# Cross-attention: other key tiles for the value jobs, and one later step of the next mask

## The chip, the cores and the metric

The kernel runs on one core of a Trainium2 chip. The metric is the time of one execution in microseconds (us), measured on the device; of the kernel before there are three such runs. "Layer 0" and "layer 1" are the two decoder layers.

## The reference, cut to what matters

The program is a two-layer pre-norm decoder on x of 4 x 512 x 256 in float32. In each layer come self-attention, cross-attention over a context of 4 x 1601 x 192, and a mixture of experts. Only the two cross-attentions are touched. In layer 0 (8 heads of 64) it is, for each batch element,

```
q = (x @ W_q).reshape(b, n, 8, 64); k, v = (context @ W_k), (context @ W_v)
sim  = einsum('bihd,bjhd->bhij', q, k) / 8
sim  = where(mask[:, None, None, :], sim, -max)
attn = softmax(sim); out = einsum('bhij,bjhd->bihd', attn, v)
return out @ W_o + b_o
```

with n = 512 queries, j = 1601 keys, and x = x + this of layernorm(x). Layer 1 is the same with 16 heads and no mask.

## The kernel before, in words

`cross(layer)` works in groups: one group is two heads of one batch element. Layer 0 has 16 groups (4 for each batch element), layer 1 has 32 (8 for each). A group runs over 13 key tiles of 128 keys (the last has 65), numbered t = 0 to 12, and a closing step t = 13. All five engines walk the same static list of groups and tiles, each in its own queue and in program order, and meet only at semaphores. There is no planner: what is done when is given by the function `at(g, t)`, which names the jobs that follow the scores of tile t in group g, and by `maxima_at`, which places the maxima.

Main work of a tile t of group g:

- TensorE makes the scores of the two heads (L1122 and L1123, two matmuls each), ScalarE takes their exponential into a ring PR (L1234), and GpSimd adds the exponentials up over the tiles into ACC (L1009), for the softmax's denominator.
- After every second tile, at even t, TensorE multiplies the exponentials of two tiles with the values V (L1139, eight matmuls at t = 2, 4, ..., 12, four at t = 13). So an even tile holds much more TensorE work than an odd one.
- In tiles 1 to 11 TensorE also makes plain scores for group g + 1 (L1075), of which VectorE takes the row maxima (L1292 in layer 0, L1295 in layer 1). The banks that hold them are few: TensorE may write the next only when VectorE has reduced an earlier one. In layer 1 an odd tile has two such pairs (one between the two heads' scores, one after the jobs), an even tile has one (after the jobs). In layer 0 every tile has three single ones (tile 4 has four).

Jobs, which share two banks in turn:

- `k` (t = 0 to 3) and `q` (t = 0) project keys and queries of group g + 1. ScalarE copies the rounded part, VectorE subtracts it (L1263, L1268, L1270), and DMAs place the parts.
- `sum` (t = 2) adds ACC over the partitions (L1047). It waits until the second last job's bank is free, which is a `k` job whose bank VectorE frees at L1263.
- `v` projects the values of four heads, two key tiles to a job: ten matmuls of 256 columns (L1039), then one copy on ScalarE (L1182). The seventh job has one key tile, five matmuls; it is called the short job below. Seven jobs serve two groups. `values_at(g)` says which a group has: four and then three in the next group, or, where a new batch element begins, none and then all seven. The last groups have none.
- `out` (t = 10, 11) projects the output of group g - 1; `row` (t = 12) turns the maxima of g + 1 into a row.
- VectorE inverts the denominators of group g - 1 (L1302, tiles 4 to 7 in layer 0, two each at tiles 5 and 7 in layer 1) and normalises at tiles 8 and 9 (L1309).

In layer 0 VectorE prepares the next batch element's mask in the second of its four groups, in four steps, `mask_step(b, c)`. Step 0 casts the columns of the mask (L1326) and then its rows, 128 x 1601 bytes to bfloat16 (L1327), and releases the DMA that loads the next rows. Step 1 reduces (L1330) and scales (L1331), step 2 makes the per-key bias and the scale of the queries (L1333, L1334), step 3 makes what is added ahead of the maxima (L1336). They are used two groups later at the earliest. Before the change step 0 stands at t = 0, and steps 1, 2, 3 at t = 11, 12, 13. That happens in groups 1, 5 and 9 of layer 0, counted from 0.

The value jobs stand at t = 4 and on, one to a tile, without a gap: three jobs at 4, 5, 6; four at 4 to 7; seven at 4 to 10.

Of the kernel before, what the change touches and what calls it, by code (L numbers as in the profile page):

```python
# [14 lines left out]
B, S, C = 4, 512, 256  # L15
# [41 lines left out]
class Core:  # L57
# [716 lines left out]
    def cross(self, layer):  # L774
# [6 lines left out]
        heads, masked = HEADS[layer], layer == 0  # L781
        pairs = heads // 2
# [14 lines left out]
        def values_at(g):  # L797

            n = g // 2 + 1  # L800
            if n >= G // 2:
                return []
            jobs = [("v", n, c) for c in range(len(VJ))]
            if 2 * n % pairs == 0:
                return jobs if g % 2 == 1 else []
            return jobs[0:4] if g % 2 == 0 else jobs[4:]

        def at(g, t):

            jobs = []  # L810
            if g + 1 < G:
                jobs += {0: [("k", g + 1, 0), ("q", g + 1, 0)], 1: [("k", g + 1, 1)], 2: [("k", g + 1, 2)],
                         3: [("k", g + 1, 3)]}.get(t, [])
            if g >= 1 and t == 2:
                jobs.append(("sum", g - 1, 0))
            if t >= 4:
                jobs += values_at(g)[t - 4:t - 3]
            if g >= 1 and t in (10, 11):
                jobs.append(("out", g - 1, t - 10))
            if g + 1 < G and t == 12:  # L820
                jobs.append(("row", g + 1, 0))
            return jobs

        after = [("sum", G - 1, 0), ("out", G - 1, 0), ("out", G - 1, 1)]
        order = before() + [("row", 0, 0)] + [x for g in range(G) for t in range(KT + 1) for x in at(g, t)] + after
        place = {x: i for i, x in enumerate(order)}

# [8 lines left out]
        def maxima_at(g, t, *at):  # L836

            return [(g + 1, *x) for w, b in zip(where, blocks) for x in b if w[0] == t and w[1] in at] if g + 1 < G else []
# [6 lines left out]
        with self.room() as sb:  # L845
# [50 lines left out]
            with self.stage() as (sem, ctx):  # L896
# [348 lines left out]
                def _(dve):  # L1245
                    steps = [0]

                    def link(ins):

                        steps[0] += 1  # L1250
                        ins.then_inc(o_step, 1)
                        dve.wait_ge(o_step, steps[0])

                    def job(x):
                        kind, g, c = x
                        i, par = place[x], g % 2
                        J = JB[i % 2]
                        if kind == "k":
                            o, w = CHUNKS[c]
                            dve.wait_ge(k_high, NC * g + c + 1)  # L1260
                            for h in range(2):
                                hd = slice(h * DH, (h + 1) * DH)
                                last = dve.tensor_tensor(KB[0:DH, par, h, o:o + w], J[hd, 0:w], KH[hd, o:o + w], ALU.subtract)  # L1263
                            last.then_inc(job_done[i % 2], 1)
                        elif kind == "q":
                            sc = qscale[:, g // pairs:g // pairs + 1]
                            dve.wait_ge(q_high, g + 1)
                            dve.scalar_tensor_tensor(QA[DH:P, par, 0, :], J[0:DH, :], sc[0:DH], QZ[0:DH, 0, :],  # L1268
                                                     ALU.mult, ALU.subtract)
                            dve.scalar_tensor_tensor(QA[0:DH, par, 1, :], J[DH:P, :], sc[DH:P], QZ[DH:P, 1, :],  # L1270
                                                     ALU.mult, ALU.subtract).then_inc(job_done[i % 2], 1)
                        elif kind == "out":
                            dve.wait_ge(job_ready[i % 2], i // 2 + 1)
                            dve.wait_ge(x_based, B * NT)
                            t = g // pairs * NT + 2 * c
                            x2 = X[:, t:t + 2, :]
                            dve.tensor_tensor(x2, J[:, :].rearrange("p (t n) -> p t n", t=2), x2, ALU.add)\
                               .then_inc(job_done[i % 2], 1)

                    def maximum(g, i, h):  # L1280

                        t, c = i % NT, i // NT
                        o, w = CHUNKS[c]
                        w = min(w, S2 - o)
                        if not masked and h == 0:
                            return
                        out = mx[:, h, t, c:c + 1]
                        dve.wait_ge(mx_ready, 2 * (NT * NC * g + i) + h + 1)
                        m = 2 * i + h
                        if masked:  # L1290
                            b = MX[(m if g == 0 else h) % 4][:, 0:w]
                            dve.tensor_tensor_reduce(b, b, maskadd[:, g // pairs % 2, o:o + w], 1.0, -BIG,  # L1292
                                                     ALU.add, ALU.max, out).then_inc(mx_done, 1)
                        else:
                            dve.tensor_reduce(mx[:, :, t, c], couples[i % 2 if g == 0 else 0][:, :, 0:w], AX.X, ALU.max).then_inc(mx_done, 1)  # L1295

                    def invert(g, i):

                        if i == 0:
                            wait_job(dve, ("sum", g, 0))  # L1300
                        part = RD[:, i * P:(i + 1) * P]
                        dve.reciprocal(part, part).then_inc(inverted, 1)  # L1302
# [8 lines left out]
                    def maxima_end(g):  # L1311
                        dve.wait_ge(mx_done, (2 if masked else 1) * NT * NC * (g + 1))
                        if g >= 1:
                            wait_ready(dve, ("row", g - 1, 0))
                        dve.tensor_reduce(MT[:, 0:8], mx[:, :, :, :].rearrange("p h t c -> p (h t) c"), AX.X, ALU.max).then_inc(m_ready, 1)

                    def mask_step(b, c):

                        if not masked:
                            if b == 0 and c == 0:  # L1320
                                dve.memset(qscale[:, :], DH ** -0.5).then_inc(prep, 1)
                            return
                        seen, scale, add = allowed[:, 0, b:b + 1], allowed[:, 1, b:b + 1], maskadd[:, b % 2, 0:S2]
                        if c == 0:
                            dve.wait_ge(self.cross_in, 32 + 16 * b)
                            link(dve.tensor_copy(keybias[:, b, :], mask_cols[:, b, :]))  # L1326
                            dve.tensor_copy(add, mask_rows[:, :]).then_inc(rows_read, 1)  # L1327
                            dve.wait_ge(rows_read, b + 1)
                        elif c == 1:
                            link(dve.tensor_reduce(seen, add, AX.X, ALU.max))  # L1330
                            link(dve.tensor_scalar(scale, seen, BIG, None, ALU.mult))  # L1331
                        elif c == 2:
                            link(dve.tensor_scalar(keybias[:, b, :], keybias[:, b, :], -1.0, scale, ALU.add, ALU.mult))  # L1333
                            dve.tensor_scalar(qscale[:, b:b + 1], seen, DH ** -0.5, None, ALU.mult).then_inc(prep, 1)  # L1334
                        else:
                            link(dve.tensor_scalar(add, add, -1.0, scale, ALU.add, ALU.mult))  # L1336
# [29 lines left out]
                    for g in range(G):  # L1366
                        for t in range(KT + 1):
                            for x in maxima_at(g, t, 0, 1, 2, 3):
                                maximum(*x)
                            if t == max(where)[0] and g + 1 < G:  # L1370
                                maxima_end(g + 1)
                            for x in at(g, t):
                                job(x)
                            if g >= 1:
                                for i in parts_at.get(t, ()):
                                    invert(g - 1, i)
                                if t in (8, 9):
                                    normalise(g - 1, t - 8)
                            if masked and g % pairs == 1 and g // pairs + 1 < B and t in (0, 11, 12, 13):
                                mask_step(g // pairs + 1, (0, 11, 12, 13).index(t))  # L1380
                    for i in range(NT):
                        invert(G - 1, i)
                        if i % 2 == 1:
# [501 lines left out]
```

## Time and profile before

| | us |
|---|---|
| median of 3 runs | 3261.02 |
| lowest, highest | 3252.44, 3264.88 |
| the profiled execution | 3253.24 |
| its span | 3251.5 |

The page of the profile gives each engine's busy time. Its view of stretches gives, for each stretch of the span that is named by its start and end, the stretch's length, and then for PE (TensorE's matmuls), PEld (its weight loads), DVE (VectorE), ACT (ScalarE) and POOL (GpSimd) the busy time in it with the number of instructions, then the mean granted clock of TensorE (1.00 is 2.4 GHz, 0.50 is 1.2 GHz), the busy share of the DMA engines and the rate. The stretches below are tiles or runs of tiles: each begins with the first score matmul (L1122) of its first tile and ends where that of the next begins, so the length of a stretch is what TensorE's queue needed for it. A timeline row gives the start, the duration, engine, line, operation and tiles, and in brackets the idle time before it and what ended that.

### The profile page before, as it was taken

How to read it: one execution, taken by the hardware profiler on the slowest of the kernel's cores; microseconds unless marked ns; L12 is line 12 of the kernel's file. 1: busy time of each engine (PE TensorE's matmuls, PEld its weight loads, DVE VectorE, ACT ScalarE, POOL GpSimd, SP SyncE). 2: the span in 40 equal slices, each digit the busy share in tenths (PEclk: the TensorE clock that was granted, in tenths of full speed). 3: DMA queues.
4: the chain of work that ended last, by engine and by line, in shares of the span. 5: the costliest groups of instructions: out<-in, count | busy, mean ns of one | idle time of the engine just before them, and what ended most of it. 6: DMA issues, size and time to landing. Idle time of an engine off the chain costs nothing. (4 is left out here: it accounts for less than half of the span.)

```text
span 3251.5 us, 38293 instructions
## 1 busy us (share of the span) xinstructions
PE 2838.1 (87%) x12634; PEld 1750.4 (54%) x12634; DVE 1856.3 (57%) x3758; ACT 1303.4 (40%) x2329; POOL 1660.1 (51%) x1408
## 2 busy tenths in 40 slices
PE   5578886999899999685799999999999999999979
PEld 5323334556565565443555656555565556556557
DVE  2456674666766665435556555555655565565546
ACT  1135554445454454120344444444444444444410
POOL 0344302666666667501366666666666666666710
PEclk8779998999999999795799999999999999999979
DMA  8666603232332321000322322322332232222110
GB/s 281 145 163 153 143 1 95 64 100 53 97 71 52 91 69 31 33 0 0 99 63 65 71 81 67 72 56 60 95 73 49 67 102 59 60 62 69 31 52 27
DMA packets 113533, 245.81 MB, mean 76 GB/s; under 512 B 15366, under 2 KB 61703, under 8 KB 112184
## 3 DMA queue, kind: packets, MB, share of 16 engines
q1 hardware_dynamic: 107128, 219.82, 27.0%
q0 software_dynamic: 5696, 23.42, 2.6%
q8 instruction: 102, 1.67, 0.2%
q14 instruction: 95, 0.78, 0.1%
q10 hardware_dynamic: 512, 0.13, 0.0%
HBM read 107.31 MB, written 31.76 MB: 43 GB/s over the span
## 5 line engine op out<-in xcount | busy, mean ns | idle before, releaser
L1009 POOL TENSOR_TENSOR ACC<-ACC,PR 128x512 f32<-128x512 f32 (+1 forms) x1056 | 1331.0, 1283 | 486.3 <-ACT PR L1234 477.3
L1234 ACT ACTIVATE PR<-banks 128x512 f32<-128x512 f32 (+1 forms) x832 | 468.8, 597 | 682.7 <-PE banks L1123 681.6
L1295 DVE TENSOR_REDUCE mx<-banks 128x2 f32<-128x800 f32 (+1 forms) x512 | 504.2, 986 | 406.5 <-PE banks L1075 405.3
L1139 PE MATMUL banks<-PR,V 128*64 128x512 f32 (+1 forms) x2496 | 602.9, 607 | 0.0
L1122 PE MATMUL banks<-QA,KA 128*128 128x512 f32 (+1 forms) x1248 | 535.5, 429 | 8.5 <-DMA QB<-ROW 7.3
L1075 PE MATMUL banks<-KH,QZ 128*128 128x400 f32 (+1 forms) x1536 | 482.9, 372 | 58.0 <-DVE mx L1295 37.8
L1123 PE MATMUL banks<-QB,KB 65*128 65x512 f32 (+1 forms) x1248 | 494.9, 397 | 0.0
L1075 PEld LDWEIGHTS banks<-KH,QZ 128*128 128x128 f32 x1536 | 268.5, 189 | 246.5 <-issue 113.9
L1234 ACT ACTIVATE PR<-banks,small 128x512 f32<-128x512 f32 (+1 forms) x416 | 269.4, 687 | 306.9 <-PE banks L1123 299.2
L1292 DVE CUSTOM_DVE_ANT_0 banks<-banks,maskadd 128x400 f32<-128x400 f32 (+1 forms) x512 | 289.8, 587 | 158.9 <-PE banks L1075 153.4
L1263 DVE TENSOR_TENSOR KB<-banks,KH 64x400 fp32r<-64x400 f32 (+1 forms) x384 | 219.4, 571 | 260.7 <-ACT KH L1167 255.2
L1122 PEld LDWEIGHTS banks<-QA,KA 128*128 128x128 f32 (+1 forms) x1248 | 231.0, 185 | 220.3 <-issue 188.9
L1139 PEld LDWEIGHTS banks<-PR,V 128*64 128x64 f32 (+1 forms) x2496 | 154.6, 137 | 262.6 <-issue 243.3
L1009 POOL TENSOR_TENSOR ACC<-PR 128x512 f32<-128x512 f32 x96 | 121.1, 1280 | 340.8 <-ACT PR L1234 340.8
L1123 PEld LDWEIGHTS banks<-QB,KB 65*128 65x128 f32 (+1 forms) x1248 | 231.5, 185 | 32.2 <-issue 11.0
L1027 PE MATMUL banks<-CX,WK 128*128 128x400 f32 (+1 forms) x960 | 220.6, 361 | 14.2 <-DVE KB L1263 6.3
L1039 PE MATMUL banks<-WV,CX 128*128 128x256 f32 (+1 forms) x1560 | 210.8, 280 | 0.0
L1039 PEld LDWEIGHTS banks<-WV,CX 128*128 128x128 f32 (+1 forms) x1560 | 204.5, 184 | 11.6
L676 ACT ACTIVATE PR<-banks 128x512 f32<-128x512 f32 x256 | 144.5, 600 | 154.9 <-DVE banks L746 127.9
L1027 PEld LDWEIGHTS banks<-CX,WK 128*128 128x128 f32 x960 | 178.5, 194 | 47.2 <-DVE QA L1270 17.7
L1302 DVE RECIPROCAL RD<-RD 128x128 f32<-128x128 f32 x192 | 172.5, 928 | 36.4 <-ACT RD L1159 35.4
L717 DVE CUSTOM_DVE_ANT_0 banks<-banks,strip 128x512 f32<-128x512 f32 x176 | 119.3, 706 | 30.5 <-PE banks L587 29.0
(241 smaller groups left out, 2975.8 us busy)
## 6 DMA issues: line engine op xcount, KB each, us to landing
KA<-KH SPq DMA_DIRECT2D x192, 400.5 KB, 6.7
CX<-ctx_split SPq DMA_DIRECT2D x8, 2403.0 KB, 10.7
WK<-wk_split SPq DMA_DIRECT2D x48, 256.0 KB, 5.7
WV<-wv_split SPq DMA_DIRECT2D x24, 512.0 KB, 3.7
QA<-QZ SPq DMA_DIRECT2D x96, 128.0 KB, 2.3
QB<-QZ SPq DMA_DIRECT2D x96, 128.0 KB, 2.3
first<-in_w_in SPq DMA_DIRECT2D x8, 1024.0 KB, 6.1
second<-in_w_out1T SPq DMA_DIRECT2D x8, 1024.0 KB, 8.8
```

Of the source, the lines that this page charges most:

```text
L1009: pool.tensor_tensor(acc, other, PR[0:r, n % RING, :], ALU.add).then_inc(summed, 1)
L1027: last = pe.matmul(J[:, 0:w], W[:, u, :], CX[:, v, o:o + w], start=(n == 0), stop=(n == 4))
L1039: last = pe.matmul(J[0:r, o:o + 2 * P], CX[:, v, t * P:t * P + r], WV[:, u, :], start=(n == 0), stop=(n == 4))
L1075: pe.matmul(bank_at[:, 0:w], QZ[:, h, t * P:(t + 1) * P], KH[:, o:o + w], start=True, stop=True).then_inc(mx_ready, 1)
L1122: pe.matmul(SB[n % 3][0:r, :], KA[:, par, h, t * P:t * P + r], QA[:, par, h, :], start=True, stop=False)
L1123: pe.matmul(SB[n % 3][0:r, :], KB[:, par, h, t * P:t * P + r], QB[:, par, h, :], start=False, stop=True).then_inc(sc_ready, 1)
L1139: last = pe.matmul(OB[h * DH:(h + 1) * DH, :], V[0:r, g % 4, s, h * DH:(h + 1) * DH], PR[0:r, (n + h) % RING, :], start=(s == 0), stop=(s ...
L1234: act.activation(PR[0:r, n % RING, :], SB[n % 3][0:r, :], ACT.Exp, bias=keybias[0:r, g // pairs, t:t + 1] if masked else 0.0).then_inc(pro ...
L1263: last = dve.tensor_tensor(KB[0:DH, par, h, o:o + w], J[hd, 0:w], KH[hd, o:o + w], ALU.subtract)
L1292: dve.tensor_tensor_reduce(b, b, maskadd[:, g // pairs % 2, o:o + w], 1.0, -BIG, ALU.add, ALU.max, out).then_inc(mx_done, 1)
L1295: dve.tensor_reduce(mx[:, :, t, c], couples[i % 2 if g == 0 else 0][:, :, 0:w], AX.X, ALU.max).then_inc(mx_done, 1)
L1302: dve.reciprocal(part, part).then_inc(inverted, 1)
```

## The change: what it does

```diff
@@ at(g, t), the jobs of a tile
-            if t >= 4:
-                jobs += values_at(g)[t - 4:t - 3]
+            todo = values_at(g)
+            for x, tile in zip(todo, {0: (), 3: (5, 7, 9), 4: (4, 5, 7, 9), 7: range(4, 11)}[len(todo)]):
+                if tile == t:
+                    jobs.append(x)
@@ VectorE's queue, at the end of a tile
-                            if masked and g % pairs == 1 and g // pairs + 1 < B and t in (0, 11, 12, 13):
-                                mask_step(g // pairs + 1, (0, 11, 12, 13).index(t))
+                            if masked and g % pairs == 1 and g // pairs + 1 < B:
+                                for c in {11: (0,), 12: (1, 2), 13: (3,)}.get(t, ()):
+                                    mask_step(g // pairs + 1, c)
```

A group with three value jobs has them at tiles 5, 7 and 9, one with four at 4, 5, 7 and 9, one with seven where they were. Mask step 0 moves from tile 0 to the end of tile 11, step 2 from tile 12 stays there behind step 1, which moves from 11 to 12, and step 3 stays at 13. The order of the jobs among themselves, and so the bank of each, stays the same.

## Rows read from the trace of the kernel before

**Rows 1.** The page: busy time of the engines, and the largest group.

```profile
PE 2838.1 (87%) x12634; PEld 1750.4 (54%) x12634; DVE 1856.3 (57%) x3758; ACT 1303.4 (40%) x2329; POOL 1660.1 (51%) x1408
...
L1009 POOL TENSOR_TENSOR ACC<-ACC,PR 128x512 f32<-128x512 f32 (+1 forms) x1056 | 1331.0, 1283 | 486.3 <-ACT PR L1234 477.3
```

**Rows 2.** Stretches, layer 1, tiles 4 to 9: group without value jobs, with three, four.

```profile
1906.36:1925.47 19.11, 16.61 (x67) 8.60 (x67) 13.74 (x16) 7.18 (x13) 15.11 (x13) 1.00 0.82 235
2048.91:2069.20 20.29, 18.81 (x93) 11.75 (x92) 13.71 (x16) 8.67 (x16) 15.14 (x13) 1.00 0.44 100
2001.26:2022.43 21.17, 20.29 (x108) 13.63 (x107) 13.72 (x16) 9.57 (x17) 15.19 (x13) 1.00 0.43 97
```

**Rows 3.** Stretches, layer 1: tile 4, 5, 9, each without and with a job.

```profile
1906.36:1910.10 3.74, 3.50 (x15) 1.36 (x15) 3.14 (x4) 1.43 (x3) 3.70 (x4) 1.00 0.66 134
2001.26:2005.70 4.44, 4.44 (x26) 2.62 (x25) 3.14 (x4) 2.02 (x4) 3.91 (x4) 1.00 0.68 139
1910.10:1912.76 2.66, 2.04 (x11) 1.51 (x9) 0.99 (x1) 1.19 (x2) 1.32 (x2) 1.00 0.97 219
2005.70:2008.65 2.95, 2.95 (x20) 2.77 (x19) 0.99 (x1) 1.36 (x3) 1.42 (x2) 1.00 1.02 232
1922.75:1925.47 2.72, 2.01 (x10) 1.51 (x9) 1.54 (x3) 1.19 (x2) 1.46 (x2) 1.00 0.40 170
1971.22:1974.17 2.95, 2.95 (x21) 2.77 (x19) 0.99 (x1) 1.37 (x3) 1.42 (x2) 1.00 0.00 0
```

**Rows 4.** Timeline, layer 1, tiles 6 and 7 without jobs: maxima after the scores.

```profile
1914.01 0.63 PE L1075 MATMUL banks<-KH,QZ 128*128 128x400 f32 x2 [0.15 <-DVE mx L1295]
...
1918.61 0.63 PE L1075 MATMUL banks<-KH,QZ 128*128 128x400 f32 x2 [0.62 <-DVE mx L1295]
```

**Rows 5.** Stretches, layer 0, tiles 4 to 9: group without value jobs, with three, four.

```profile
871.32:890.59 19.27, 16.34 (x69) 9.04 (x68) 15.31 (x44) 8.31 (x13) 13.95 (x12) 1.00 0.80 235
824.85:844.84 19.99, 18.96 (x93) 12.16 (x93) 15.32 (x44) 9.78 (x16) 13.97 (x12) 1.00 0.45 103
772.35:793.06 20.71, 20.45 (x108) 14.07 (x108) 15.42 (x44) 10.70 (x17) 14.04 (x12) 1.00 0.44 99
```

**Rows 6.** Stretches, layer 0: tile 4, 5, 9, each without and with a job.

```profile
871.32:876.44 5.12, 4.01 (x17) 1.91 (x17) 3.46 (x10) 1.85 (x3) 3.42 (x3) 1.00 0.69 140
772.35:777.48 5.13, 5.13 (x28) 3.21 (x28) 3.45 (x10) 2.45 (x4) 3.44 (x3) 1.00 0.69 140
876.44:878.97 2.53, 1.75 (x9) 1.23 (x9) 2.33 (x6) 1.34 (x2) 1.02 (x1) 1.00 1.01 235
777.48:780.13 2.65, 2.65 (x18) 2.47 (x18) 2.46 (x7) 1.34 (x2) 1.15 (x1) 1.00 0.99 232
888.58:890.59 2.01, 1.75 (x9) 1.23 (x8) 1.81 (x6) 1.26 (x2) 0.96 (x2) 1.00 0.14 57
936.62:939.28 2.66, 2.66 (x18) 2.46 (x18) 2.01 (x7) 1.34 (x2) 1.14 (x1) 1.00 0.00 0
```

**Rows 7.** Stretches, layer 0: tile 2 of groups 1, 5, 9 and 2.

```profile
615.96:627.56 11.60, 8.47 (x25) 3.24 (x25) 6.53 (x12) 3.43 (x7) 5.71 (x4) 0.71 0.20 46
809.76:821.73 11.97, 8.77 (x26) 3.28 (x25) 6.59 (x12) 3.43 (x7) 5.72 (x4) 0.71 0.19 45
1003.58:1014.20 10.62, 7.44 (x26) 3.07 (x26) 6.59 (x12) 3.44 (x7) 5.70 (x4) 0.84 0.22 51
...
667.85:674.22 6.37, 5.86 (x26) 2.75 (x26) 3.98 (x10) 3.45 (x7) 4.97 (x4) 1.00 0.38 85
```

**Rows 8.** Timeline, group 1 of layer 0: the cast, then the sum job.

```profile
617.62 2.03 DVE L1327 CAST maskadd<-mask_rows 128x1601 bf16<-128x1601 uint8 x1
...
621.39 1.97 PE L1047 MATMUL banks<-ACC,ones 128*64 128x512 f32 x4 [3.13 <-DVE KB L1263]
```

**Rows 9.** VectorE's timeline after mask step 3, end of group 9.

```profile
1051.49 0.57 DVE L1263 TENSOR_TENSOR KB<-banks,KH 64x400 fp32r<-64x400 f32 x1 [2.57 <-ACT KH L1167]
```

**Rows 10.** Instructions that read the mask's rows: shortest, median, longest in ns.

```profile
L1327 DVE CAST maskadd<-mask_rows x4: 999/2023/2026, 527.6 to 1005.3; 128x1601 bf16<-128x1601 uint8 x4
```

## The prediction

> **What bounds the kernel now.** First the page: matmuls are busy for 87% of the span, more than any other engine, VectorE for 57% and GpSimd for 51% [rows 1]. That is an average. To see what a moved job is worth I cut the cross-attention into tiles with the view of stretches and compared groups that differ only in their number of value jobs. A layer 1 group without value jobs takes 19.11 us for tiles 4 to 9, of which matmuls fill 16.61; three jobs make it 20.29 and four 21.17 with matmuls busy for 20.29 [rows 2]. Layer 0 shows 19.27, 19.99 and 20.71 [rows 5]. So a stretch without jobs has some 2.5 us (19.11 - 16.61) in which TensorE stands still, and a job costs less than its own length where it falls into such a hole.
>
> What is in the hole: the timeline of a layer 1 group without jobs shows TensorE waiting 0.62 us in the odd tile in front of the second maxima, and 0.15 us in the even tile, each time until VectorE has reduced the maxima before [rows 4]. At an odd tile a value job stands exactly in front of that wait. An even tile has the long value product behind it, in which VectorE catches up, and little to fill.
>
> Last I looked for tiles that are unlike their neighbours. Tile 2 takes 6.37 us in layer 0, but 11.60, 11.97 and 10.62 in groups 1, 5 and 9, at a mean granted clock of 0.71, 0.71 and 0.84 [rows 7]. Those are the three groups in which mask step 0 is at tile 0. The timeline shows its cast of 2.03 us on VectorE and, behind it, the sum job on TensorE after 3.13 us of idle, released by L1263, which had queued behind the cast [rows 8].
>
> **Value jobs, layer 1.** Price of a full job by tile, from pairs with and without [rows 3]: tile 4, 4.44 - 3.74 = 0.70; tile 5, 2.95 - 2.66 = 0.29; tile 9, 2.95 - 2.72 = 0.23. Tile 7 has the same work as tile 5 (two inversions on VectorE), so I take 0.29. The short job at tile 9 has half the matmuls. A full job there turned 2.01 us busy and 0.71 idle into 2.95 without idle, so it added 0.94 of busy time; half of that, 0.47, is less than the idle 0.71, and I take 0.
> - Three jobs: 19.11 + 0.29 + 0.29 + 0 = 19.69, against 20.29: 0.60 saved.
> - Four jobs: 19.11 + 0.70 + 0.29 + 0.29 + 0.23 = 20.62, against 21.17: 0.55 saved.
> - Counted from `values_at`: 32 groups; the pairs 6 and 7, 14 and 15, 22 and 23 carry 0 and 7 jobs and stay as they are, groups 30 and 31 have none, and 12 groups have four and 12 have three. 12 x 0.60 + 12 x 0.55 = 13.8 us.
>
> **Value jobs, layer 0.** Prices [rows 6]: tile 4, 5.13 - 5.12 = 0.01 (four maxima keep VectorE the slower there); tile 5, 2.65 - 2.53 = 0.12, taken for tile 7 too; tile 9, 2.66 - 2.01 = 0.65. The short job at tile 9, from two sides: the full one added 0.91 of busy time, half is 0.46 against 0.26 idle, which leaves 0.20; and if a full job is 1.19 long (worked out below), the tile with half of it is 2.66 - 0.60 = 2.06, which is 0.05 more than without. I take 0.1.
> - Three jobs: 19.27 + 0.12 + 0.12 + 0.1 = 19.61, against 19.99: 0.38 saved, in 4 groups.
> - Four: 19.27 + 0.01 + 0.12 + 0.12 + 0.65 = 20.17, against 20.71: 0.54 saved, in 4 groups.
> - 4 x 0.38 + 4 x 0.54 = 3.7 us. Both layers: 17.5 us.
>
> What the rows do not show is a full job in an odd tile behind an even tile without one; in every group of before, jobs stand in neighbouring tiles. Bounds for it: at best it costs nothing, at worst its whole length. The whole length is what tile 6 of layer 0 paid: 20.71 - 19.27 = 1.44 for four jobs, less 0.01, 0.12 and 0.12 for tiles 4, 5 and 7, is 1.19. I take the middle rows' price, since in layer 1 the wait that it fills [rows 4] is counted from the odd tile's own first maxima, whatever stood in the tile before, and since VectorE is busy 13.7 of 19.1 us in these tiles [rows 2], 15.3 of 19.3 in layer 0 [rows 5], with or without jobs.
>
> What else a value job issues: its copy on ScalarE, which is at 40% [rows 1] and follows two tiles later at most; no DMA. The queues: SyncE's load of the next value weights waits for the last value job, but in front of that, in the same queue, it waits for the `out` job of tile 11, so tile 9 in place of 6 delays nothing. The first use of these values is in the next group but one at the earliest. `out` at tile 10 follows a value job at tile 9 in the seven-job groups already.
>
> **Mask step 0.** Against group 2, VectorE is busy 6.53 - 3.98 = 2.55 us longer in tile 2 of group 1, TensorE idle (11.60 - 8.47) - (6.37 - 5.86) = 2.62 us longer, and the rest, 5.23 - 2.62 = 2.61, is the same matmuls at the lower clock: 0.71 is a mean of 1.2 and 2.4 GHz [rows 7], and what TensorE did before it fell is the 3.13 us of idle [rows 8]. Tile 2 should go back to 6.37: 5.23 + 5.60 + 4.25 = 15.1 us.
>
> At its new place, behind the `out` job of tile 11, VectorE's queue holds only steps 1 to 3 and then L1263 of the next group. In group 9, whose idle is the shortest I found of the three, VectorE then stood idle for 2.57 us until ScalarE's copy let it go on [rows 9]. Step 0 costs 2.62, so L1263 is late by 0.05 there and nowhere else. Bounds: 0 and, with the cover gone, 2.62 each, 7.9 in all; and should TensorE's clock fall again, the whole 15.1 is lost. I take 0.1. `maxima_end` and `out`, on which TensorE waits, stand in front of the step. It issues no DMA; the one that it releases (the rows of the next mask) is wanted two groups later. GpSimd's adds may wait for the cast, but its next customer is the sum at tile 2 of the next group.
>
> The cast took 2.03 us in the three groups and 1.00 us in the set-up, where GpSimd has no adds [rows 10]. By that rule the cast at tile 11 costs 1.00 plus the rest of one add, at most 1.00 + 1.28 = 2.28 with the add of [rows 1], and the sum would lose up to 0.3 us more for each of three groups, so 31.6 in place of 32.5.
>
> **Sum.** 17.5 + 15.1 - 0.1 = 32.5 us. The profiled execution took 3253.24, its span 3251.5 and 1.7 around it: 3220.7. That execution was near the lowest of the runs (3252.44); the median is 7.8 above it. Since the tiles outside the change keep whatever made that difference, I subtract from the median: 3261.0 - 32.5 = 3228.5, and say 3228. About 0.5%, 16 us, is what can be told from no change.
>
> **The rivals.**
> - *A: value jobs gain about half or less, mask all.* VectorE's two inversions behind tile 5 or 7 could hold up the next first maxima once the even tile is shorter, and the wait moves to where no job stands. For it: the even tile shrinks by 0.70 of 4.44 [rows 3]. Against: groups without any job run these tiles at 19.11 [rows 2], with the shortest even tiles there are. The value part would be 0 to 9 us; time 3261 - 15 - 4.5 = 3241.
> - *B: mask step only moved.* L1263 comes late at the start of groups 2, 6 and 10 and TensorE idles there, and its clock falls. Against: the 2.57 us [rows 9]. Time 3261 - 17.5 = 3243.
> - *C, slower: the odd tiles 7 and 9 give no cover.* A full job there costs 1.19 and a short one 0.6, because VectorE, not the maxima's order, sets the tile. Then layer 1 has 19.11 + 0.29 + 1.19 + 0.6 = 21.19 for three jobs, 0.90 more than now, and 19.11 + 0.70 + 0.29 + 2.38 = 22.48 for four, 1.31 more: 26.5 us over 24 groups. Layer 0 has 21.18 and 21.78, 1.19 and 1.07 more, 9.0 us. With the mask's 15.1 off, +20: 3281. Linear between this (+35.5 for the value part) and my prices (-17.5), it outweighs the mask from about 0.8 us for a job at tile 7 or 9. Against: tile 9 with a job in the seven-job groups, 2.95 and 2.66 [rows 3, 6].
> - *D: more.* The short jobs vanish wholly and the tile 9 jobs cost what tile 5 does: a few us more, and with an execution like the lowest, 3214.
>
> **How the numbers follow.** Forecast 0.68, A 0.14, B 0.06, C 0.03, D 0.09. The likeliest's own range is 3220 to 3237, the width of the three runs around it. A's 3241 and B's 3243 on one side, D on the other give 3213 to 3245 as the range. Faster by over 0.5% means under 3244.7: forecast, D, nearly all of A and more than half of B, 0.92. Within 0.5%: 0.05. Slower: 0.03.
>
> The Trainium skill, "TensorE: Matmul & The Clock Gate", Part 1, says that the window by which the clock is set runs free of the kernel, so that its cost varies between runs. The trace agrees in that the same extra idle cost 5.23, 5.60 and 4.25 us in all [rows 7]. By the rule the mask part could be anything from the idle alone, 3 x 2.62 = 7.9, up; the sum by that is 25.3 and lies inside the range.
>
> **What would show it.** In the changed trace: tiles 4 to 9 at 19.7 and 20.6 us in layer 1 and at 19.6 and 20.2 in layer 0 for three and four jobs; tile 2 of groups 1, 5 and 9 at 6.4 with clock 1.00; L1263 at the start of groups 2, 6, 10 with nearly no idle before it; seven-job groups unchanged. The prediction is wrong if odd tiles with a job take over 3.3 us in layer 1, or if a clock below 1.00 shows up inside layer 0 where there was none.

## The result, and the profile after

The changed kernel takes 3222.55 us (median of 6 runs, 3217.87 to 3228.53), the kernel before 3259.51 (6 runs, 3252.44 to 3264.88): ratio 0.9889, 95% interval 0.9873 to 0.9904. That is 36 us less by the ratio (31 to 41), 37 by the medians; forecast were 32.5, and 3228. The two profiled executions are 3253.24 and 3217.87, 35.4 apart.

Stretches of the changed kernel, columns as in [rows 2]: tiles 4 to 9, in layer 1 without value jobs, with three, with four; then the same in layer 0.

```profile
1878.62:1897.74 19.12, 16.62 (x68) 8.60 (x68) 13.73 (x16) 7.19 (x13) 15.10 (x13) 1.00 0.81 235
2020.62:2040.32 19.70, 19.04 (x93) 11.74 (x92) 13.71 (x16) 8.68 (x16) 15.16 (x13) 1.00 0.46 104
1973.49:1994.11 20.62, 20.30 (x108) 13.63 (x107) 13.71 (x16) 9.15 (x17) 15.38 (x14) 1.00 0.43 99
857.39:876.65 19.26, 16.33 (x69) 9.05 (x68) 15.31 (x44) 8.32 (x13) 13.97 (x12) 1.00 0.81 235
811.35:830.92 19.57, 18.44 (x93) 12.12 (x93) 15.37 (x44) 9.57 (x15) 14.08 (x12) 1.00 0.46 105
765.01:785.19 20.18, 20.18 (x108) 14.06 (x108) 15.51 (x45) 10.18 (x16) 14.71 (x12) 1.00 0.45 102
```

Against [rows 2, 5] the groups without jobs did not move, three jobs went from 20.29 to 19.70 and from 19.99 to 19.57, four from 21.17 to 20.62 and from 20.71 to 20.18. Matmuls of a four-job group in layer 1 are busy as long as before (20.30 against 20.29); it is the idle between them that went.

Stretches of the changed kernel: tile 2 of groups 1, 5, 9 and 2 of layer 0, beside [rows 7].

```profile
614.29:620.65 6.36, 5.86 (x26) 2.76 (x25) 3.98 (x10) 3.45 (x7) 4.99 (x4) 1.00 0.36 84
801.90:808.24 6.34, 5.84 (x25) 2.74 (x25) 3.97 (x10) 3.44 (x7) 4.98 (x4) 1.00 0.37 85
989.05:995.40 6.35, 5.85 (x25) 2.76 (x25) 3.98 (x10) 3.46 (x7) 4.97 (x4) 1.00 0.37 85
660.12:666.50 6.38, 5.88 (x26) 2.75 (x26) 4.00 (x10) 3.47 (x7) 4.99 (x4) 1.00 0.37 85
```

The 11.60, 11.97 and 10.62 us are all 6.35 now, at clock 1.00. VectorE's timeline of the changed kernel, from the end of group 1 into group 2, beside [rows 9], shows the moved step and what was left of the cover:

```profile
651.71 0.17 DVE L1328 CAST small<-mask_cols 128x13 f32<-128x13 uint8 x1
651.90 1.98 DVE L1329 CAST maskadd<-mask_rows 128x1601 bf16<-128x1601 uint8 x1
...
656.30 0.63 DVE L1338 TENSOR_SCALAR maskadd<-maskadd,allowed 128x1601 bf16<-128x1601 bf16 x1
657.51 1.16 DVE L1265 TENSOR_TENSOR KB<-banks,KH 64x400 fp32r<-64x400 f32 x2 [0.57 <-ACT KH L1169]
```

(L1265 is L1263 of before.) 0.57 us of idle is left here, 0.82 and 0.81 after the two later steps, so nothing came late.

Where the 35.4 us of the two profiled executions are, tile by tile over all 48 groups: tiles 4 to 9 of layer 1 13.5, of layer 0 3.5, tile 2 of groups 1, 5 and 9 15.1. The remaining tiles of the two cross-attentions give back 1.3, 0.8 of it at tile 12, where a group's length depends on when a small DMA lands (in one group of layer 1 TensorE waited 1.18 us for it, and the tile was 1.25 us longer). That makes 30.8. The other 4.5 lie outside: the stage between the cross-attentions, which the change does not touch, was 4.3 us shorter, the start 1.4 shorter, the end 1.1 longer. In the profiles below that middle stretch took 295.3 to 300.5 us and the start 563 to 574, with no relation to the variant. So the change is worth 30.8 us as far as its tiles show it. That lies at the lower edge of the 31 to 41 of the ratio; whether the rest of the 36 is chance is not shown.

### The profile page after: what moved, and what is told of

Read it like the earlier page. It is cut to its first block and busy times, and to the rows that moved or that the text cites. A ratio compares the mean times of both kernels' runs of the same rounds, so it can differ in the third digit from the quotient of the medians.

```text
span 3216.1 us, 38290 instructions
## 1 busy us (share of the span) xinstructions
PE 2828.9 (88%) x12634; PEld 1747.4 (54%) x12634; DVE 1858.5 (58%) x3758; ACT 1305.0 (41%) x2329; POOL 1662.3 (52%) x1408
## 5 line engine op out<-in xcount | busy, mean ns | idle before, releaser
L1265 DVE TENSOR_TENSOR KB<-banks,KH 64x400 fp32r<-64x400 f32 (+1 forms) x384 | 219.5, 572 | 255.1 <-ACT KH L1169 249.5
L1041 PE MATMUL banks<-WV,CX 128*128 128x256 f32 (+1 forms) x1560 | 211.0, 280 | 0.0
L1041 PEld LDWEIGHTS banks<-WV,CX 128*128 128x128 f32 (+1 forms) x1560 | 204.5, 184 | 11.6 <-DVE KB L1265 0.2
```

Source lines behind the costliest of these rows:

```text
L1041: last = pe.matmul(J[0:r, o:o + 2 * P], CX[:, v, t * P:t * P + r], WV[:, u, :], start=(n == 0), stop=(n == 4))
```

## The experiments

All but one are edits of the changed kernel, in which the lines of the jobs stand two further on than before (L1265 for L1263, L1041 for L1039, L1049 for L1047); an edit that adds a line shifts them by one more. Where a line of an edit is long, "..." marks what is left out of it here. The kernel before ran beside each set; its medians there were 3257.2, 3257.0, 3255.3 and 3258.7.

**One half at a time.** Mask steps moved, value jobs at the old tiles:

```diff
-            todo = values_at(g)
-            for x, tile in zip(todo, {0: (), 3: (5, 7, 9), 4: (4, 5, 7, 9), 7: range(4, 11)}[len(todo)]):
-                if tile == t:
-                    jobs.append(x)
+            if t >= 4:
+                jobs += values_at(g)[t - 4:t - 3]
```

> Only the mask steps move, the value jobs stay at tiles 4 and on. Theory (the two halves add up, each acts through its own tiles): 15 us less than before, tile 2 of groups 1, 5 and 9 at 6.4 us, all other tiles as before; ratio 0.9954. Rival (the mask step costs only its 2.6 us of queue time, the clock would have fallen anyway): 8 us less. Rival (the gain of the whole change is the value jobs' alone): no difference.

Measured 3241.2 us, ratio 0.9944 (0.9924 to 0.9965): 18 less than before, 11 to 25, by the ratio. Tile 2 of groups 1, 5 and 9 together lost 15.1 us, tiles 4 to 9 lost 0.2. So the rival that gave the mask step 8 us falls too.

Value jobs moved, mask steps at tiles 0, 11, 12, 13. This run is the kernel before with the first half of the change alone, the lines in `at(g, t)`.

> Only the value jobs move, mask step 0 stays at tile 0. Theory: 17.5 us less than before, ratio 0.9946, tile 2 of groups 1, 5 and 9 still at 10.6 to 12 us with a granted clock under 1. Rival (the halves overlap, since TensorE is slack after the mask step): 20 us or more. Together with the run with the mask alone it should make up the 32.5 forecast, or show whether the 35 to 37 us measured come from inside the cross-attention at all.

Measured 3236.7, ratio 0.9933 (0.9908 to 0.9957): 22 less, 14 to 30. Tiles 4 to 9 lost 17.2 us (13.6 and 3.6). Tile 2 of the three groups took 11.87, 10.53 and 12.05 us, together 34.5 against 34.2 before, though group 5 was 1.4 shorter and group 9 1.4 longer: TensorE stood idle 3.13, 3.20 and 3.18 us in front of the sum in both kernels, but how long the clock then stayed low changed between the groups. In the tiles that they touch the halves add up to the whole; by the ratios they make 40 against 36, within the intervals. The 22 alone would also fit the rival of "20 us or more", and it is the tiles that speak against it. The rivals that gave all to one half fall.

**Even tiles.** The same number of jobs, spread out as widely, but at even tiles:

```diff
-            for x, tile in zip(todo, {0: (), 3: (5, 7, 9), 4: (4, 5, 7, 9), 7: range(4, 11)}[len(todo)]):
+            for x, tile in zip(todo, {0: (), 3: (4, 6, 8), 4: (4, 6, 8, 10), 7: range(4, 11)}[len(todo)]):
```

> The changed kernel with the value jobs at the even tiles: three at 4, 6, 8 and four at 4, 6, 8, 10. Theory (a job costs what its tile's idle time does not cover): an even tile charges 0.76 us in layer 1 and 1.17 in layer 0 (0.70 and 0.01 at tile 4, about 1.1 at tile 10), so three jobs cost 0.5 more than at 4, 5, 6 in layer 1 and 1.1 more in layer 0, four jobs 1.3 and 2.1 more: 34 us more than the old places, so about 51 more than the changed kernel, 3274, and 19 more than before in spite of the mask's 15. Rival (what matters is that jobs are spread out, with a free tile between them): like the changed kernel within 5 us, 3222.

Measured 3273.6, ratio 1.0056 (1.0039 to 1.0072), slower than before: 18 us by the ratio (13 to 23), where the prices said 19. Stretches of this kernel, tiles 4 to 9 of layer 1, three jobs and four (the fourth is at tile 10, outside):

```profile
2056.91:2077.63 20.72, 18.78 (x92) 11.72 (x92) 13.74 (x16) 8.65 (x16) 15.13 (x13) 1.00 0.43 98
2007.88:2029.23 21.35, 19.41 (x97) 12.37 (x97) 13.75 (x16) 8.98 (x16) 15.14 (x13) 1.00 0.43 96
```

The three-job group has the work of the changed kernel, but 20.72 - 18.78 = 1.9 us of idle stay in the odd tiles. Being spread out is worth nothing; the tile is what counts. "With a free tile between them" falls.

**Is the hole the wait for the maxima?** In layer 1 VectorE reduces 2 x 16 scores in place of 2 x 400, with the new tiles and with the old. The kernels leave out the rest of the maxima, and so layer 1's scores are scaled to a thousandth:

```diff
-    dve.tensor_reduce(mx[:, :, t, c], couples[i % 2 if g == 0 else 0][:, :, 0:w], AX.X, ...
+    dve.tensor_reduce(mx[:, :, t, c], couples[i % 2 if g == 0 else 0][:, :, 0:16], AX.X, ...
...
-                                dve.memset(qscale[:, :], DH ** -0.5).then_inc(prep, 1)
+                                dve.memset(qscale[:, :], DH ** -0.5 / 1000).then_inc(prep, 1)
```

> The changed kernel with VectorE's maxima of layer 1 over 2 x 16 in place of 2 x 400 scores (left out: the rest of the maxima, and the scores of layer 1 are scaled to a thousandth). The reduction then takes some 0.1 to 0.2 us and TensorE should hardly wait for it. To be read against the same with the value jobs at their old places. Theory (the odd tiles' gain is the wait for the maxima): that gain of 13.8 us in layer 1 goes, so the two differ by layer 0's 3.7 us, 2 to 6. Rival (the gain comes from the jobs being away from the long value product, or from ScalarE's and GpSimd's pace): they still differ by 16 to 18.

> The same short maxima in layer 1, mask steps as changed, value jobs at the old places (4, 5, 6 and 4 to 7). Theory: in layer 1 a full job costs its whole length, 1.17 us, in tiles 4, 5, 6 and 7 alike, and the whole kernel is only 2 to 6 us slower than the short-maxima kernel with the new places. Rival: 16 to 18 us slower, with prices by tile as in the kernel before (0.70, 0.29, 0.76, 0.29).

Measured 3134.5 (new tiles) and 3146.9 (old). Stretches with the new tiles: group of layer 1 without jobs and with three, tiles 4 to 9; tile 5 without and with a job. Then the old tiles, three jobs.

```profile
1861.77:1877.16 15.39, 15.39 (x68) 8.84 (x67) 6.41 (x16) 6.83 (x13) 14.42 (x13) 1.00 0.89 250
1995.37:2013.37 18.00, 18.00 (x92) 11.95 (x92) 6.90 (x16) 8.46 (x16) 14.96 (x13) 1.00 0.50 114
...
1865.02:1866.88 1.86, 1.86 (x11) 1.51 (x9) 0.19 (x1) 0.77 (x2) 1.01 (x2) 1.00 0.94 186
1954.84:1957.80 2.96, 2.96 (x21) 2.78 (x20) 0.19 (x1) 1.36 (x3) 1.43 (x2) 1.00 1.00 230
```

```profile
2010.71:2028.97 18.26, 18.26 (x93) 11.81 (x92) 6.43 (x16) 8.29 (x16) 14.43 (x13) 1.00 0.49 111
```

Without the wait a group without jobs takes 15.39 in place of 19.11, and the job at tile 5 costs 2.96 - 1.86 = 1.10 in place of 0.29, with nearly the same 2.95 us for the tile. The gain of the new tiles in tiles 4 to 9 of layer 1 falls from 13.5 to 4.5 us. So the wait for the maxima was two thirds of it. The rest was not expected. By tile it is a difference of price that is left with the short maxima: a full job costs 1.18 us at tiles 4 and 6, 1.10 at 5 and 7 and 1.03 at tile 9, and the short job 0.60 at tile 6 and 0.43 at tile 9. Why an odd tile is the cheaper one even then is open. The two medians differ by 12.5, between the 2 to 6 of the theory and the rival's 16 to 18; in the profiled executions the two cross-attentions differ by 9.6, of which layer 0 has 3.5. Layer 0's own gain was not put to such a test: that its hole too is the wait for the maxima is argued, not shown.

**How the price of the mask step comes about.** The cast of the columns and a part of that of the rows, 400 values or 800 of 1601, back at tile 0, the rest at tile 11. The edit for 400, shortened:

```diff
+                            else:
+                                link(dve.tensor_copy(add[:, 0:400], mask_rows[:, 0:400]))
...
+                        elif c == 4:
+                            dve.tensor_copy(add[:, 400:S2], mask_rows[:, 400:S2]).then_inc(rows_read, 1)
...
-                                for c in {11: (0,), 12: (1, 2), 13: (3,)}.get(t, ()):
+                                for c in {0: (0,), 11: (4,), 12: (1, 2), 13: (3,)}.get(t, ()):
```

> The changed kernel, but with the cast of the mask's columns and of 400 of the 1601 mask values back at tile 0; the other 1201 stay at tile 11. Theory (cost is VectorE's queue time, plus TensorE's lower clock once its idle is long enough): TensorE's idle in front of the sum grows from 0.50 by the length of the two casts, 0.9 to 1.7 us with the wait for one GpSimd add, to under 2.3; tile 2 takes 7.3 to 8.1, and if the clock stays at 1.00 the cost is 3 to 5 us in all. Rival (the clock is not tied to the length of this idle): tile 2 rises by the same again for the clock, to 9 or more, clock under 0.9.

> The same with 800 of the 1601 values at tile 0. Theory: idle in front of the sum 1.9 to 2.7 us, tile 2 at 7.8 to 8.5 without the lower clock and 10 to 11 with it; it lies between 5 and 13 us above the changed kernel. Rival (the cost grows in proportion to the values cast at tile 0): half of 15, 7.5 us, with no step between a quarter and the whole.

Measured 3233.5, ratio 0.9927 (0.9906 to 0.9949), and 3236.3, ratio 0.9934 (0.9910 to 0.9958). Tile 2 of group 1 with a quarter, and of groups 1 and 5 with the half:

```profile
619.18:629.12 9.94, 7.43 (x26) 3.06 (x26) 5.91 (x12) 3.44 (x7) 5.09 (x4) 0.83 0.23 54
```

```profile
616.62:626.68 10.06, 7.36 (x26) 3.07 (x26) 6.11 (x12) 3.44 (x7) 5.30 (x4) 0.83 0.23 53
808.15:819.70 11.55, 8.78 (x25) 3.28 (x25) 6.18 (x12) 3.45 (x7) 5.30 (x4) 0.70 0.20 45
```

My bound of 2.3 us for the idle failed: it was 9.94 - 7.43 = 2.51 with a quarter, and the tile and its clock came out as the rival had them; since the bound was overrun, this does not decide between the rival's reason and mine. The clock was under 1.00 in all six tiles. With a quarter of the cast at tile 0 the three groups took 10.8 us more than in the changed kernel, with the half 12.9, with the whole 15.1: most of the price is there with the first part, and the rival of "half of 15" falls. The instructions that read the mask's rows, with the quarter at tile 0 and then with the half (ns: shortest, median, longest), say why:

```profile
L1332 DVE CAST maskadd<-mask_rows x3: 1390/1395/1401, 620.8 to 1002.5; 128x400 bf16<-128x400 uint8 x3
L1335 DVE CAST maskadd<-mask_rows x3: 777/779/780, 660.2 to 1041.7; 128x1201 bf16<-128x1201 uint8 x3
...
L1332 DVE CAST maskadd<-mask_rows x3: 1604/1604/1607, 618.3 to 1002.5; 128x800 bf16<-128x800 uint8 x3
L1335 DVE CAST maskadd<-mask_rows x3: 569/570/573, 657.7 to 1042.1; 128x801 bf16<-128x801 uint8 x3
```

At tile 0 the cast of 800 values takes 1.60 us, at tile 11 that of 801 takes 0.57: 1.03 on top. The whole takes 2.03 and 1.00 [rows 10], again 1.03 on top. For 400 values the difference is about 1.04, if 0.36 is taken for the casting itself (an estimate, on the line through 0.57 for 801 and 0.78 for 1201). It is a wait, not a slower cast.
**How much cover the end of a group has.** The cast at tile 11 made three times:

```diff
+                            for _ in range(2 if b else 0):
+                                link(dve.tensor_copy(add, mask_rows[:, :]))
```

> The changed kernel with the cast of the mask rows made three times at tile 11 (the two extra results are overwritten by the same). In the changed trace VectorE stands idle for 0.57 to 0.81 us between mask step 3 and L1265 of the next group. Theory (that idle is the cover, and nothing in front of it waits): the two extra casts take 1.0 each if GpSimd is between adds and up to 2.0 if not, 2.0 to 4.0 together, so L1265 comes 1.2 to 3.4 us late in groups 2, 6 and 10, and tiles 0 to 2 of those groups get longer by that, more where the granted clock falls: 4 to 15 us in all. Rival (VectorE at the end of a group has cover of its own further on, the late L1265 is absorbed by waits in tiles 0 to 2 that are there anyway): under 2 us in all.

Measured 3230.4, ratio 0.9922 (0.9900 to 0.9944). Stretches: tiles 1 and 2 of group 2, of group 6, of group 10 (2.44 and 6.38 in the changed kernel).

```profile
667.79:672.22 4.43, 2.72 (x13) 1.95 (x12) 4.23 (x9) 2.63 (x4) 1.59 (x2) 1.00 0.26 59
672.22:677.88 5.66, 5.66 (x26) 2.84 (x26) 3.20 (x9) 2.87 (x5) 3.46 (x3) 1.00 0.21 50
856.42:861.66 5.24, 3.14 (x12) 2.36 (x11) 4.90 (x9) 2.73 (x5) 2.40 (x2) 0.91 0.35 81
861.66:868.45 6.79, 6.79 (x26) 3.73 (x24) 2.92 (x8) 2.89 (x5) 2.64 (x3) 0.82 0.06 14
1046.75:1051.46 4.71, 2.71 (x13) 1.94 (x12) 4.51 (x9) 2.63 (x4) 1.87 (x2) 1.00 0.30 72
1051.46:1058.63 7.17, 7.17 (x26) 3.97 (x25) 3.20 (x9) 2.98 (x5) 3.15 (x3) 0.76 0.12 28
```

TensorE idles 1.71, 2.10 and 2.00 us in tile 1. In group 2 the clock stayed at 1.00, and tile 2 got 0.7 shorter, 0.5 of it its own idle, which was used up: 1.3 us in all. In groups 6 and 10 the clock fell, and it was 3.2 and 3.1. So the cover is real, it is short, and what lies beyond it is dear: 7.5 us in three groups, within the 4 to 15 forecast.

**Filling more holes.** One job of a group at tile 1:

```diff
-            for x, tile in zip(todo, {0: (), 3: (5, 7, 9), 4: (4, 5, 7, 9), 7: range(4, 11)}[len(todo)]):
+            for x, tile in zip(todo, ({0: (), 3: (4, 5, 7), 4: (1, 4, 5, 7), 7: (1, 4, 5, 6, 7, 9, 11)} if masked else
+                                  {0: (), 3: (1, 5, 7), 4: (1, 5, 7, 9), 7: (1, 4, 5, 6, 7, 9, 11)})[len(todo)]):
```

> The changed kernel with more jobs in holes: layer 0 three jobs at 4, 5, 7 and four at 1, 4, 5, 7; layer 1 three at 1, 5, 7 and four at 1, 5, 7, 9; seven at 1, 4, 5, 6, 7, 9, 11 in both. At tile 1 the job stands before the last key job but one and so before the wait in front of the sum, which is 1.04 us in layer 1 and 0.50 in layer 0. Theory: a job at tile 1 costs 0.15 in layer 1 and 0.7 in layer 0 instead of 0.70 (tile 4) and 0.65 (tile 9); four-job groups of layer 1 save 0.55 each, 6.6 us; three-job groups of layer 1 save nothing or 0.3; seven-job groups save some 0.9 each, 5 us; in all 10 to 14 us less than the changed kernel, 3210. Rival (the sum's wait is on VectorE's queue in itself, and the job only stands in front of key work that VectorE then gets later): no gain or up to 10 us slower than the changed kernel.

Measured 3305.4, ratio 1.0145 (1.0116 to 1.0174), 83 us slower than the changed kernel where 10 to 14 less were forecast: my theory was wrong there, and the rival's "up to 10 us slower" was too small. TensorE's timeline of tiles 1 and 2 in a layer 1 group:

```profile
1659.59 1.45 PE L1042 MATMUL banks<-WV,CX 128*128 128x256 f32 x10 [1.18 <-DVE QA L1273]
...
1663.67 1.17 PE L1030 MATMUL banks<-CX,WK 128*128 128x400 f32 x5 [1.33 <-DVE KB L1266]
```

Two banks serve all jobs in turn, and I had counted holes without counting banks. At tile 1 the value job takes the bank of the `q` job, which VectorE frees late, and the next `k` job then waits for another. The 1.04 us of idle in front of the sum is gone, but 1.18 and 1.33 stand in its place, and the job is there as well: tiles 1 and 2 of layer 1 together take 12.2 us in place of 9.2.

**The sum job a tile later**, by the same rule read the other way: let the job whose bank is late stand back.

```diff
-            if g >= 1 and t == 2:
+            if g >= 1 and t == 3:
                 jobs.append(("sum", g - 1, 0))
```

> The changed kernel with the sum job moved from tile 2 to tile 3, behind the last key job. At tile 2 TensorE stands idle for 1.04 us in layer 1 and 0.50 in layer 0 until VectorE has freed the bank of the key job before the last; at tile 3 the same bank is long free, and the sum waits for a key job that is one tile older. Theory (a wait for a bank, as in the run that put value jobs at tile 1 and paid 2.6 us each for it, goes when the job stands a tile later): tile 2 shorter by 2.0 in layer 1 (the idle and the sum's own 1.0), tile 3 longer by 1.0; 31 x 1.0 + 15 x 0.5 = 38 us less than the changed kernel at best, 25 to 38 expected, about 3190. Rival (the idle moves on to tile 3 or to the inversions of tile 4 in layer 0, which then start late): within 5 us of the changed kernel.

Measured 3209.2, ratio 0.9863 (0.9842 to 0.9885), 13 less than the changed kernel instead of 25 to 38. The profiled execution was the lowest of the five, 3199.9, and by tile its two cross-attentions are 22.9 us shorter: 15.8 in layer 0, where 7.5 were forecast, and 7.1 in layer 1, where 31 were. Layer 1 groups with three jobs and none got 1.0 us shorter as expected. Those with four or seven did not: their first value job at tile 4 now waited for the bank of the last `k` job. TensorE's timeline at tile 4 of such a group, and the stretch of tile 4 in another:

```profile
1963.31 1.44 PE L1041 MATMUL banks<-WV,CX 128*128 128x256 f32 x10 [1.35 <-DVE KB L1265]
```

```profile
2146.87:2154.43 7.56, 6.21 (x26) 3.65 (x24) 3.13 (x4) 1.91 (x4) 2.62 (x3) 0.77 0.98 212
```

The idle of 1.35 us stands in fourteen groups, those with four or seven jobs but the first. In thirteen of them the clock stayed at 1.00 and tile 4 took 6.05 us; in this one it fell.

**And no job at tile 4 of layer 1**, on top of the sum at tile 3:

```diff
-            for x, tile in zip(todo, {0: (), 3: (5, 7, 9), 4: (4, 5, 7, 9), 7: range(4, 11)}[len(todo)]):
+            for x, tile in zip(todo, ({0: (), 3: (5, 7, 9), 4: (4, 5, 7, 9), 7: range(4, 11)} if masked else
+                                  {0: (), 3: (5, 7, 9), 4: (5, 6, 7, 9), 7: range(5, 12)})[len(todo)]):
```

> The sum job at tile 3 as before, and in layer 1 no value job at tile 4, where with the sum at 3 it waited 1.35 us for the last key job's bank: four at 5, 6, 7, 9 and seven at 5 to 11. Theory (prices by tile: 0.29, 0.76, 0.29, 0.23 at tiles 5, 6, 7, 9): a four-job group of layer 1 takes 44.64 + 0.29 + 0.76 + 0.29 + 0.23 = 46.2 us from its first score to the next group's, in place of 47.75 with the sum alone moved and 47.15 in the changed kernel; 12 of them save 18.5 us against the sum alone moved, the three of seven jobs 1 each; in all 20 us less than it, about 3189. Rival (the wait at tile 4 moves to tile 5 with the job): the same as with the sum alone moved, 3209.

Measured 3186.4, ratio 0.9765 (0.9742 to 0.9789): 36 us less than the changed kernel by the medians, and 77 less than before by the ratio (69 to 84; 72 by the medians). A four-job group of layer 1, first score to first score, in the kernel with the sum alone moved and then in this one (47.15 in the changed kernel):

```profile
1946.65:1994.39 47.74, 45.61 (x215) 28.72 (x213) 27.32 (x35) 21.45 (x39) 30.16 (x24) 1.00 0.25 57
```

```profile
1948.35:1994.54 46.19, 45.32 (x215) 28.79 (x213) 27.31 (x35) 21.45 (x39) 30.20 (x24) 1.00 0.26 59
```

46.2 was forecast from the prices by tile. Against the sum alone moved, the four-job groups together give 18.8 us and the seven-job groups 3.6, where 18.5 and 3 were forecast. The profiled execution lost some of it again in the last group. VectorE's multiply that normalises the output there (L1312), TensorE's next `out` job, GpSimd's adds, and the stretch of tile 10:

```profile
L1312 DVE TENSOR_TENSOR OT<-OT,RD x96: 361/495/16348, 647.6 to 3048.5; 128x256 f32<-128x256 f32 x96
3031.03 2.04 PE L1057 MATMUL banks<-WO,OT 128*128 128x256 f32 x4 [7.20 <-issue]
3008.42 22.22 POOL L1012 TENSOR_TENSOR ACC<-ACC,PR 128x512 f32<-128x512 f32 x18
3022.62:3036.21 13.59, 6.39 (x17) 2.43 (x15) 9.33 (x3) 1.92 (x4) 8.02 (x7) 0.62 0.01 1
```

This multiply began within 0.01 us of an add and ended only after thirteen adds back to back, 16.35 us later, and tile 10 took 13.59 us in place of 3.86. In the other profiles no such multiply takes more than 1.6. Whether it happened in the other executions of this kernel too is not known, and why in this one is open.

## Why the prediction was right

- *Prices by tile.* 0.60 and 0.55 us a group were forecast for layer 1 (measured 0.59 and 0.55), 0.38 and 0.54 for layer 0 (0.42 and 0.53, by the stretches above). In sum 17.5 forecast, 17.0 measured in tiles 4 to 9. The combination that the rows did not show, a job at an odd tile behind an even tile without one, costs what it did elsewhere: with a job, tiles 5, 7 and 9 of layer 1 take 2.93 to 2.96 us whatever stood in the tile before.
- *The short job at tile 9.* 0 and 0.1 us; measured 0 (2.72, as without) and 0.06 (2.07 against 2.01).
- *Where the hole comes from.* The short maxima show the wait for VectorE to be two thirds of layer 1's gain. I had taken it for all. The sum did not depend on it, since it went by groups with and without jobs. For layer 0 the cause is not shown.
- *Mask step.* 15.1 forecast, 15.1 measured in those three tiles. That it agrees so well owes something to both being read against one profile of the kernel before; in the run with the value jobs alone the same tiles would have given 15.4, in another order. The half that was put down to the clock is borne out by group 2 of the run with three casts, which idled 1.7 us without a lower clock and lost 1.3, against 3.1 to 3.2 for 2.0 and 2.1 us of idle with one.
- *The cover at the end of the group.* 2.62 of cost against 2.57 of idle, late by 0.05; in fact 0.6 to 0.8 us stayed. The term mis-sized is step 0's cost at its new place. The cast itself took 1.98, inside the 2.28 of the bound. But the cast of the columns took 0.17 in place of 0.53, and step 2's small one 0.23 in place of 0.57. In the trace the former falls on the seam between two of GpSimd's adds, and the latter comes after GpSimd's last add of the group has ended (655.00), while before it began in the midst of one. I had not counted that the neighbours get cheaper too. The sign that I gave, nearly no idle in front of the next group's first L1263, was wrong by as much.
- *Rivals.* A (half the value gain) and B (the mask step only moved) fall by tile. C fell: odd tiles charge 0.23 to 0.29 in layer 1. A price like C's 1.19 appears only with the short maxima (1.03 to 1.10), because no hole is left there. D's reason, still cheaper jobs, did not come true either: tile 9 charges 0.23 us in layer 1 and 0.66 in layer 0, nearly what was forecast. The 4.5 us between 30.8 and the profiled 35.4 lie in stages whose length varies as much between variants that leave them alone.
- *What was luck.* The tiles that were priced gave 32.1 of the 32.5 forecast, but the remaining tiles took 1.3 back, which I had put at nothing, and the measured 36 is reached only with time outside the change. The mechanism accounts for 30.8 us; the other 5 were not forecast, and their cause is open.

## What to carry to other kernels

Where engines walk a static list in step, cut the trace at the step's first instruction and compare steps that differ in one job: the differences are prices, and they include every hidden wait. They added up as long as no job changed which bank another waits for: for the even tiles 3274 was forecast from them and 3273.6 measured. Where the banks changed partners they failed, by some 95 us for the jobs at tile 1 and by 12 to 25 for the sum at tile 3. For the last kernel 3189 was forecast and 3186.4 measured, but the closeness is in part luck, since its profile holds 9.7 us in the last group that no price has. Before a job goes into an idle stretch, follow the bank or buffer that it will take: idle behind a late bank cannot be filled by a job that takes a late bank as well. And a long instruction on a helper engine costs more than its length where the main engine's clock falls around the idle that it makes; put it where the queue behind it is empty.

## What the runs showed of the hardware that was not expected

A cast of 128 x 400 bytes to bfloat16 on VectorE that began 0.1 us behind one of GpSimd's adds took 1.40 us, more than one of 128 x 1201 that began 0.06 us ahead of one (0.78): cutting a colliding instruction to a quarter saved 0.63 of 2.03 us.

A multiply of 128 x 256 on VectorE, 0.5 us in the median, once took 16.35 us beside GpSimd's adds: it did not come between any two of thirteen adds that followed each other without a pause.

TensorE's granted clock, in the mean of the tile, was between 0.70 and 0.91 around each of the idle stretches of 2.1, 2.5, 2.7 and 3.1 us in the middle of dense work, and after one of 2.00 the tile behind it had 0.76. After the one of 1.71 it stayed at 1.00. But it was 0.77 around one of the fourteen stretches of 1.35 us, and 1.00 around the other thirteen: a shorter idle is no safe one.
